# A graph network block on one core: the second attention layer's scores from weights times q and k, and an earlier fetch of swapped queries

## The reference, cut to what matters

```python
def _gate(h, q, Wg, bg, Wq, bq):
    ...
    attn = sigmoid(hg[:, :, None, :] + qg[:, None, :, :])      # hg: nodes, qg: queries
    qi = einsum('bnlf,blf->bnf', attn, q)
    alpha = sigmoid(h3 @ Wq[:, :F].T + qi @ Wq[:, F:].T + bq)
    return alpha * tanh(qi) + (1.0 - alpha) * h3

def rgat_conv(x, W, q, k, b, src, dst, etype, heads, out_ch, n_nodes):
    xr = einsum('nd,rdf->rnf', x, W)                           # three relations
    oi, oj = xr[etype, dst], xr[etype, src]
    alpha = leaky_relu(oi @ q + oj @ k, 0.2)
    a = softmax of alpha over the edges of each dst
    out = segment_sum(a * oj, dst)
    return out + b

h = elu(rgat_conv(x, W1, q1, k1, b1, ..., heads=4))
out = rgat_conv(h, W2, q2, k2, b2, ..., heads=1)
```

## Time and profile before

| | us |
|---|---|
| median of 3 runs | 279.88 (279.55 to 280.65) |
| the profiled execution's own time | 279.16 |
| its span in the trace | 277.4 |
| PE busy in the span | 255.4 (92%) |
| DVE busy | 146.9 (53%) |
| ACT busy | 91.6 (33%) |
| POOL busy | 85.5 (31%) |
| mean granted clock of TensorE | 0.994 of full speed |

### The profile page before, as it was taken

How to read it: one execution, slowest core, us unless ns; L and a number is a source line. 1 busy time by engine, 2 the same in 40 slices (tenths; PEclk the granted TensorE clock), 3 DMA queues, 4 the chain that set the end, 5 groups by cost and what they waited for, 6 DMA issues and landing times.

```text
span 277.4 us, 4929 instructions
## 1 busy us (share of the span) xinstructions
PE 255.4 (92%) x2073; PEld 132.2 (48%) x2073; DVE 146.9 (53%) x261; ACT 91.6 (33%) x155; POOL 85.5 (31%) x74
## 2 busy tenths in 40 slices
PE   8799999999899989899976998889999988998994
PEld 4566854455345532467752322225554443434572
DVE  1744640018999999730041999994632236114423
ACT  2312520034759986120001666771311022003000
POOL 7680000003999999100000668770000000000000
PEclk9999999999999999999997999999999999999999
DMA  7999996993007938004999600005999062000001
GB/s 238 374 402 402 402 390 195 409 401 121 1 0 263 402 95 270 0 2 144 408 296 392 239 4 2 0 2 169 377 405 398 18 233 110 0 2 0 2 0 28
DMA packets 21607, 52.67 MB, mean 190 GB/s; under 512 B 4169, under 2 KB 4937, under 8 KB 21586
## 3 DMA queue, kind: packets, MB, share of 16 engines
q1 hardware_dynamic: 20896, 52.04, 51.5%
q10 hardware_dynamic: 690, 0.34, 0.5%
HBM read 51.39 MB, written 0.20 MB: 186 GB/s over the span
## 4 chain that ended last, share of the span: by engine, by line
PE 54%; POOL 16%; DVE 10%; DMA 8%; issue 6%; ACT 4%; SPq 1%; DVEq 0%; POOLq 0%; ACTq 0%
POOL prod L591 12%; PE ps L1037 10%; PE ps L1069 9%; PE ps L1185 6%; PE ps L1457 6%; DMA W<-qg 4%; POOL W L591 4%; PE ps L1011 4%; PE ps L1084 4%; DMA W<-in_L_gnn_Wg 4%; PE ps L1154 2%; ACT pre L668 2%; DVE prod L877 2%; DVE pre L885 2%; PE ps L1275 2%
## 5 line engine op out<-in xcount | busy, mean ns | idle before, releaser
L591 POOL TENSOR_TENSOR prod<-pre,qn 128x768 f32<-128x768 f32 x28 | 56.0, 2021 | 17.0 <-ACT pre L668 16.9
L885 DVE TENSOR_TENSOR pre<-ps,qg 128x768 f32<-128x768 f32 x46 | 42.9, 949 | 7.4 <-PE ps L1261 6.3
L668 ACT ACTIVATE pre<-pre 128x768 f32<-128x768 f32 x46 | 38.7, 847 | 11.9 <-DVE pre L885 11.1
L1185 PE MATMUL ps<-W 128*128 128x384 f32 x96 | 34.4, 489 | 0.2 <-ACT W L443 0.2
L443 ACT COPY W<-ps 128x384 f32<-128x384 f32 x41 | 18.3, 482 | 38.9 <-PE ps L1011 38.7
L668 ACT ACTIVATE ps<-ps 128x768 f32<-128x768 f32 x18 | 14.3, 794 | 35.0 <-PE ps L1261 26.9
L1275 PE MATMUL ps<-prod,rsel 128*32 128x384 f32 x192 | 20.5, 496 | 3.4 <-POOL prod L591 2.5
L1185 PEld LDWEIGHTS ps<-W 128*128 128x128 f32 x96 | 17.4, 190 | 9.9 <-issue 0.9
L1069 PE MATMUL ps<-W,prod 128*64 128x256 f32 (+1 forms) x240 | 20.6, 328 | 0.0
L1011 PE MATMUL ps<-ident,W 128*128 128x128 f32 x144 | 19.3, 275 | 1.2 <-ACT W L443 0.7
L1011 PEld LDWEIGHTS ps<-ident,W 128*128 128x128 f32 x144 | 16.6, 141 | 4.7 <-issue 2.0
(11 more groups left out here) (203 smaller groups left out, 321.5 us busy)
## 6 DMA issues: line engine op xcount, KB each, us to landing
W<-in_L_gnn_W SPq DMA_DIRECT2D x9, 2304.0 KB, 11.8
W<-in_L_gnn_W_rel SPq DMA_DIRECT2D x6, 2304.0 KB, 15.3
W<-in_L_gnn_W_root SPq DMA_DIRECT2D x2, 2304.0 KB, 9.9
W<-in_L_gnn_Wq SPq DMA_DIRECT2D x4, 1152.0 KB, 7.9
W<-in_L_gnn_Wg SPq DMA_DIRECT2D x3, 1152.0 KB, 13.5
qn<-in_L_gnn_query_embs SPq DMA_DIRECT2D x4, 384.0 KB, 10.4
W<-in_L_gnn_Wg SPq DMA_DIRECT2D x3, 384.0 KB, 3.9
W<-qg SPq DMA_DIRECT2D x2, 384.0 KB, 10.9
```

The source lines that it names most:

```text
L591: nc.gpsimd.tensor_tensor(prod_of(T), pre_of(T), qn[:, pair_and_node(t)[0], :], ALU.mult).then_inc(prod_p, 1)
L668: nc.scalar.activation(tile, tile, ACT.Sigmoid).then_inc(sig_ready, 1)
L885: nc.vector.tensor_tensor(dst, ring(T), by_half(qg[:, pair_and_node(T % TILES)[0], :]), ALU.add).then_inc(pre_ready, 1)
L1185: ins = nc.tensor.matmul(ps[:, unit_bank(u), 0:HD], qT[:, k, p * P:(p + 1) * P], WgT_q[:, k, c * HD:(c + 1) * HD], start=(k == 0), stop=(k ...
```

## The change

Three things change.

- **Swapped queries.** SP fetches `qs` after the first relation of the second round (`rgcn_done` of 5), ahead of `L2_W1_0` and `L1_W`, where before it came behind both and waited for a value of 7. For this `L2_W1_1` (and so `qs`) moves to slot 3, and `L1_W` and `L3_W1` to slot 5.
- **Weights times q and k made ahead.** The scores of RGAT layer 2 need x W_r q and x W_r k. The kernel now makes V = (W_r q, W_r k), 36 columns of 128 numbers (three relations, six row blocks, q or k), while the work between the second gate and RGAT layer 2 runs. Once the second gate is reduced, SP spreads the rows q2 and k2 over 128 partitions (`qk_rows`, 384 KB each). 22 columns are made by POOL, which multiplies a weight block [128, 768] by the spread row (into one of four buffers `vprod`), and ACT, which sums it (`sum_products`, five stages of 6, 4, 5, 2 and 5). 14 are made by DVE in one instruction each (`v_units`, four stages of 4, 3, 5 and 2). The two small strided transfers of q2 and k2 go.
- **RGAT layer 2.** It is written out after a loop that now runs once. PE waits for V, multiplies it with `nodeT` and has q and k terms without `XT`; the scores and the softmax then run between the parts of the projection. The attention product is added in PSUM to bias and input (`RGAT2`), half by half, and the statistics are read from there.

```diff
-            ("L1_W", 3, 1), ("L2_W1_0", 2, 1), ("L2_W1_1", 5, 1), ("L2_W1_2", 6, 1),
-            ("L2_W2_0", 4, 1), ("L2_W2_1", 0, 1), ("L2_W2_2", 1, 1), ("L3_W1", 3, 1), ("L3_W2", 2, 1)]
+            ("L1_W", 5, 1), ("L2_W1_0", 2, 1), ("L2_W1_1", 3, 1), ("L2_W1_2", 6, 1),
+            ("L2_W2_0", 4, 1), ("L2_W2_1", 0, 1), ("L2_W2_2", 1, 1), ("L3_W1", 5, 1), ("L3_W2", 2, 1)]
...
+        V = prod[:, 3, 0:KC * R * GN].rearrange("p (k r c) -> p k r c", k=KC, r=R)
+        vprod = [pre[:, 2, :], pre[:, 3, :], prod[:, 0, :], prod[:, 1, :]]
 
         ps = ctx.enter_context(nc.psum_tensor("ps", [P, 8, 512], F32))
...
+        V_OF = {r: [(r, k, c) for k in range(KC) for c in range(2)] for r in range(R)}
+        ON_VECTOR = (4, 8, 2)
+        V_VECTOR = [V_OF[r][2 * KC - ON_VECTOR[r] + i] for r in range(R) for i in range(ON_VECTOR[r])]
+        V_POOL = [V_OF[r][i] for r in range(R) for i in range(2 * KC - ON_VECTOR[r])]
+        V_VECTOR_AT = (4, 3, 5, len(V_VECTOR) - 12)
+        V_SCALAR_AT = (6, 4, 5, 2, len(V_POOL) - 17)
+
+        def v_cell(unit):
+            r, k, c = unit
+            return V[:, k, r, c:c + 1]
+
+        def v_weights(unit):
+            r, k, c = unit
+            return W[SLOT[f"L2_W2_{r}"]][:, k, :]
...
-                sp.dma_start(qk[:, :, 1, q:q + 1], halves(a[f"L2_gnn_{name}2"]),
-                             allow_slow_non_contiguous=True).then_inc(qk_loaded, 16)
             done = R + 1
-            load("L1_W", a["L1_gnn_W"], rgcn_done, done + 1)
-            load("L2_W1_0", a["L2_gnn_W1"][0], rgcn_done, done + 2)
-            sp.wait_ge(rgcn_done, done + 3)
+            sp.wait_ge(rgcn_done, done + 1)
             for c in range(2):
                 sp.dma_start(qs[c * N:(c + 1) * N, :, :],
                              qg[(1 - c) * N:(2 - c) * N, :, c * HD:(c + 1) * HD]).then_inc(qs_loaded, 16)
+            load("L2_W1_0", a["L2_gnn_W1"][0], rgcn_done, done + 2)
+            load("L1_W", a["L1_gnn_W"], rgcn_done, done + 3)
             load("L2_W1_2", a["L2_gnn_W1"][2], rgcn_done, done + 4)
             load("L2_W2_0", a["L2_gnn_W2"][0], hg_done, 2)
-            load("L2_W1_1", a["L2_gnn_W1"][1], reduced, TILES)
+            sp.wait_ge(reduced, TILES)
+            for c, name in enumerate(("q", "k")):
+                sp.dma_start(qk_rows[c], a[f"L2_gnn_{name}2"].rearrange("f o -> o f").to_broadcast([P, D])).then_inc(qk_rows_loaded, 16)
+            load("L2_W1_1", a["L2_gnn_W1"][1])
...
+            pool.wait_ge(reduced, TILES)
+            nc.gpsimd.memset(prod[:, 3, 0:KC * R * GN], 0.0).then_inc(v_cleared, 1)
+            pool.wait_ge(qk_rows_loaded, 32)
+            for i, unit in enumerate(V_POOL):
+                wait_loaded(pool, f"L2_W2_{unit[0]}")
+                if i >= len(vprod):
+                    pool.wait_ge(v_sum_s, i - len(vprod) + 1)
+                nc.gpsimd.tensor_tensor(vprod[i % len(vprod)], v_weights(unit), qk_rows[unit[2]], ALU.mult).then_inc(v_product, 1)
...
+            def sum_products(stage):
+
+                for _ in range(V_SCALAR_AT[stage]):
+                    i = summed[0]
+                    act.wait_ge(v_cleared, 1)
+                    act.wait_ge(v_product, i + 1)
+                    nc.scalar.activation(vprod[i % len(vprod)], vprod[i % len(vprod)], ACT.Copy,
+                                         accum_out=v_cell(V_POOL[i])).then_inc(v_sum_s, 1)
+                    summed[0] = i + 1
+
...
+            sum_products(1)
...
+            sum_products(2)
...
+            sum_products(3)
...
+            sum_products(4)
...
+            def v_units(stage):
+
+                for _ in range(V_VECTOR_AT[stage]):
+                    unit = V_VECTOR[v_done[0]]
+                    dve.wait_ge(v_cleared, 1)
+                    dve.wait_ge(qk_rows_loaded, 32)
+                    wait_loaded(dve, f"L2_W2_{unit[0]}")
+                    if v_done[0]:
+                        dve.wait_ge(v_sum_v, v_done[0])
+                    nc.vector.tensor_tensor_reduce(vscratch[:, :], v_weights(unit), qk_rows[unit[2]], 1.0, 0.0,
+                                                   ALU.mult, ALU.add, v_cell(unit)).then_inc(v_sum_v, 1)
+                    v_done[0] += 1
+
             blocks_out(nodeT, node_turned, nodeT_ready, 3)
+            v_units(0)
             projection_norm(wide(GCN), xa[:, :], 2, 1)
...
+                v_units(1)
...
+                v_units(2)
...
+            blocks_out(nodeT, node_turned, nodeT_ready, 5)
+            v_units(3)
+            dve.wait_ge(rel_done, 4)
+            nc.vector.tensor_copy(X2[:, 0:HD], ps[0:N, 2, 0:HD]).then_inc(X_out_v, 1)
...
+            dve.wait_ge(rel_done, 7)
+            nc.vector.tensor_copy(X01[:, HD + CUT:D], wide(X1_WIDE)[:, CUT:HD]).then_inc(X_out_v, 1)
+            for part in range(2):
+                dve.wait_ge(att_part, part + 1)
+                stats(wide(RGAT2), part)
+            layer_norm(wide(RGAT2), xa[:, :], 3)
...
-                if layer == 1:
-                    ins = add_nodes(xa, ADDEND)
...
+            turn_nodes(hx, ident, node_turned, made=(x_ready, 4))
+            keep_warm(1, 4)
+            keys = [f"L2_W2_{r}" for r in range(R)]
+            project(nodeT, W[SLOT[keys[2]]], 2, waits=as_copied(nodeT_ready, 5)).then_inc(rel_done, 1)
...
+            def project_two(out_cols, bank, cols, blocks, last):
+
+                for k in blocks:
+                    h, j = k // JC, k % JC
+                    for r in range(2):
+                        ins = nc.tensor.matmul(bank[r * N:(r + 1) * N, out_cols], nodeT[:, j, h * N:(h + 1) * N],
+                                               W[SLOT[keys[r]]][:, k, cols], start=(k == BY_BLOCK[0]), stop=(k == BY_BLOCK[-1]),
...
+            first_half(BY_BLOCK[:2])
+            nc.tensor.matmul(ps[:, SCORE2, 0:n], ident[:, :], maskb[:, :], start=True, stop=False, skip_group_check=True)
+            pe.wait_ge(v_sum_s, len(V_POOL))
+            pe.wait_ge(v_sum_v, len(V_VECTOR))
+            for k in range(KC):
+                g, h, j = k % (P // GN), k // JC, k % JC
+                for r in range(R):
+                    ins = nc.tensor.matmul(ps[g * GN:(g + 1) * GN, QK2, r * N:(r + 1) * N], V[:, k, r, :],
+                                           nodeT[:, j, h * N:(h + 1) * N], start=(k == g and r == 0),
+                                           stop=(k + P // GN >= KC), skip_group_check=True)
+            ins.then_inc(qk_done, 1)
+            first_half(BY_BLOCK[2:4])
+            pe.wait_ge(qkT_ready, 2)
+            for half in range(2):
+                nc.tensor.matmul(ps[half * N:(half + 1) * N, SCORE2, 0:n], qsel[:, 1:2].to_broadcast([P, N]), QKT,
+                                 start=False, stop=False, skip_group_check=True)
+            for r in range(R):
+                for half in range(2):
+                    ins = nc.tensor.matmul(ps[half * N:(half + 1) * N, SCORE2, r * N:(r + 1) * N], QKT[:, r * N:(r + 1) * N],
+                                           qsel[:, 0:1].to_broadcast([P, N]), start=False, stop=True, skip_group_check=True)
+            ins.then_inc(score_done, 1)
+            first_half(BY_BLOCK[4:], True)
+            add_bias_wide("L2_gnn_b2", RGAT2)
+            add_nodes_wide(xa, RGAT2)
...
+            pe.wait_ge(wts_ready, 3)
+            nc.tensor.transpose(ps[:, WT1[0], 0:P], wts[:, 0:P], ident[:, :])
+            nc.tensor.transpose(ps[0:N, WT2[0], 0:P], wts[:, P:n], ident[:, :]).then_inc(wts_turned, 1)
+            second_half(0, BY_BLOCK[4:], True)
+            second_half(1, BY_BLOCK[:3])
+
+            def attend(half, part):
+
+                cols = PARTS_OF[part]
+                at = slice(half * HD + cols.start, half * HD + cols.stop)
+                for wT, X in ((wT1, X01), (wT2, X2)):
+                    ins = nc.tensor.matmul(wide(RGAT2)[half * N:(half + 1) * N, cols], wT[:, half * N:(half + 1) * N], X[:, at],
+                                           start=False, stop=(wT is wT2), skip_group_check=True)
+                return ins
+
+            pe.wait_ge(wT_out_s, 4)
+            pe.wait_ge(wT_out_v, 2)
+            pe.wait_ge(X_out_v, 3)
+            pe.wait_ge(X_out_s, 4)
+            for part in range(2):
+                attend(0, part)
+            second_half(1, BY_BLOCK[3:], True)
+            pe.wait_ge(X_out_s, 5)
+            attend(1, 0).then_inc(att_part, 1)
+            pe.wait_ge(X_out_v, 4)
+            attend(1, 1).then_inc(att_part, 1)
```

More of the change, by code:

```diff
@@ L141, in gnn_kernel @@
         RGCN2, HG1, GCN, LAST = 6, 4, 6, 4
+        X1_WIDE, RGAT2, QK2, SCORE2 = 6, 4, 5, 3
         SCORE = (0, 2)
@@ new lines, in _ @@
+            nc.scalar.copy(score[:, n:2 * n], ps[:, SCORE[1], 0:n]).then_inc(score_out, 1)
+            for h in range(2):
+                act.wait_ge(shifted, h + 1)
+                nc.scalar.activation(expd[:, h * n:(h + 1) * n], leaky[:, h * n:(h + 1) * n], ACT.Exp,
```

(19 more changed lines are left out.)

100 lines of the change are left out of this document (58 added, 42 removed).

## The result

The changed kernel takes 291.37 us (median of 4 executions, 290.97 to 291.57) against 280.26 for the kernel before beside it: a ratio of 1.0394, 95% interval 1.0361 to 1.0427. The forecast of 290.8 with its turns between POOL and DVE is what came. The profiled execution had 291.23 with a span of 289.4, which is 12.0 above the span before.

The account below looks back on a forecast made before the run. PE was taken to carry most of the chain, handing over in places, as in its 4.14 us wait for qs. 19.4 us lost less 8.5 gained is 10.9 slower than 279.16, plus 0.7 for the median: 290.8, range 278 to 298.

Parts of the forecast that it names:

- turns between POOL and DVE: Behind the second gate: whichever engine comes second waits for the other's whole instruction; 19.4 us lost, chance 0.70, range 285 to 297.
- Swapped queries: Before the second gate: PE's wait for qs (4.1 us) and its cold start go; 5.0 us gained, bounds 4.1 to 5.3.
- RGAT layer 2: Projection's start to last statistics: PE runs through, softmax hidden, 19.8 us where it was 23.3; 3.5 gained, bounds 2.5 to 4.5.
- step 5: Softmax of RGAT layer 1 and last stage: POOL's buffers are full, the last sums end before PE needs V; +0.
- Unhindered units: DVE's units without waiting for POOL: 0.7 us for the four units and 0.2 for the five.
- Step 1: First norm: L918 and L924, twice each, wait for POOL's first four products; 5.0 late or 0, taken as 3.5 us.
- Step 2: Four units behind the first norm's last copy, 2.55 us each between products after the first; +5.7 us, 0.7 without waiting.
- Step 3: Three units in the 3.82 us idle before the X2 copy: 2.4 too much, PE's other pairs hide part; +1.0 us.
- Step 4: Five units in the 5.03 us idle before RGAT layer 1's QKT copy take 12.7; +7.7 us, 0.2 without waiting.
- Step 6: PE idles over 5 us at the four and the five units, then runs some 3 us at half clock each; +1.5 us.
- No turns: Rival: units and short DVE instructions run at their own pace beside POOL; 272.3 us, chance 0.16; decided by units under 1.3.
- Mildly placed turns: Rival: rows land too late to hit the first norm and half the units meet no product; 279 to 283 us, chance 0.14.

Follow-up runs that it names:

- swap_only: The kernel before with only the early fetch of the swapped queries (new slots and SP's new order): 273.76 us, ratio 0.9754 to the kernel before.
- no_products: The changed kernel with each of POOL's 22 products replaced by a memset of one column, most of V wrong: 271.38 us, ratio 0.9668.
- no_units: The changed kernel without DVE's 14 units, 14 columns of V zero, POOL's products and ACT's sums kept: 281.02 us, ratio 1.0024.
- psum_row: The changed kernel with the second input of DVE's 14 units read from a PSUM bank, their columns of V wrong: 281.7 us, ratio 1.0041.
- half_units: The changed kernel with 7 of DVE's 14 units (2, 1, 3 and 1 per stage), 7 columns of V zero: 284.36 us, ratio 1.0166.
- softmax_pause: The changed kernel without DVE's units, and POOL waits before its 20th product until RGAT layer 1's softmax weights are ready: 279.67 us, ratio 1.0004.
- late_fills: The changed kernel with more filling matmuls on PE before the second norm's mean and RGAT layer 1's q and k terms: 289.92 us, ratio 1.0341.
- write_only: The changed kernel with each POOL product replaced by two memsets that write but read no SBUF, 22 columns of V zero: 271.62 us, ratio 0.9683.
- late_products: The changed kernel with POOL's products started only after the first norm has written both blocks, nothing left out: 288.91 us, ratio 1.0300.

## Why the prediction was right

Four kernels (before, swap_only, no_products and the changed one) can be set against each other on DVE's timeline. Each row counts from one milestone to the next, the first from the start of the span: the end of the first norm's aggregate (L861, L800 before), the end of `nodeT`'s last copy for L1 and for RGAT layer 1, the start of the `X2` copy, of the `QKT` copy and of `hx`, and the end of the span.

| us | before | swap_only | no_products | changed | turns |
|---|---|---|---|---|---|
| to the first aggregate | 197.50 | 192.03 | 192.30 | 194.70 | +2.4 |
| to `nodeT` for L1 | 3.41 | 3.40 | 3.40 | 6.49 | +3.1 |
| to `nodeT` for RGAT 1 | 8.44 | 8.43 | 8.77 | 14.70 | +5.9 |
| to `X2` | 3.82 | 3.83 | 3.83 | 5.88 | +2.1 |
| to `QKT` | 11.88 | 11.87 | 12.55 | 17.65 | +5.1 |
| to `hx` | 8.21 | 8.22 | 7.90 | 9.14 | +1.2 |
| to the end | 44.14 | 44.12 | 40.85 | 40.84 | 0.0 |
| span | 277.4 | 271.9 | 269.6 | 289.4 | +19.8 |

The last column is changed less no_products: what the turns cost, with what the clock makes of them. It was forecast at 18.5 (19.4 less the 0.9 of unhindered units).

- **Swapped queries**, forecast −5.0 with bounds of 4.1 and 5.3: −5.5 by the spans, just outside (and 6.6 by the medians, swap_only). PE asks for `qs` without a wait, and the node terms start at 145.71 where 145.8 was worked out.
- **RGAT layer 2**, forecast −3.5: −3.3 (44.14 to 40.84). The attention in two halves took 3.45 in the chain, forecast 3.7. From the projection's start to the third norm's statistics it is 19.6 us (249.90 to 269.54; 19.8 forecast); V was complete 2.5 us before PE asked for it (DVE's last unit ended at 253.2, V's product started at 255.7), so step 5's second half held.
- **Unhindered units**, forecast +0.9: +1.0. The span of no_products is 2.3 under that of swap_only, where layer 2 gives 3.3.
- **Step 1, the first norm**, forecast +3.5: +5.5, the largest loss beyond the forecast. The rows landed 5.6 us after their issue and not 3.9, so POOL's first product spared L979 and L985 the first time round, and the aggregate lost 2.4 only. But L871 behind it lost 2.6 (3.24 for two in place of 0.67). The step counted the instructions with two SBUF inputs and left out this one, which goes from SBUF to SBUF with one tensor input. That L871 was hit is chance of timing. In no_units, psum_row, half_units, softmax_pause and late_fills the rows landed earlier, three or four of the four were held up, and POOL had no free buffer when L871 came, so it took 0.67. The norm's last copy still came 4.5 us (softmax_pause) to 6.7 us (no_units) after that of no_products: the step's size holds on the whole, and which instructions pay for it changes with when the rows land.
- **Step 2, four units**, forecast 5.0 above unhindered ones: +5.9. Each took 2.29 to 2.60, and the four with their spaces 10.1 us; 9.4 was the sum, since it let the first one slip in after 1.6.
- **Step 3, three units**, forecast +1.0: +2.1. The copy of `X2` was expected 2.4 late, and came 2.1 late: the first unit took 0.95 and the two others 2.49 each with their spaces, against 1.05 and twice 2.55. The step then let PE, busy with other work, hide 1.4 of it. That happened in late_fills, where 1.2 are made good between `X2` and `XT`; in the changed kernel PE itself came out of its idle time at the lower clock, took 5.94 for the projection that takes 4.0, and hid nothing. ACT's copy of the same result, which has no unit before it, could not start before 221.77 either: the slow projection alone would have cost as much as the units did.
- **Step 4, five units**, forecast +7.5 above unhindered ones: +5.1. The five took 10.9 us in place of 12.7, since the first one came ahead of a product and took 1.03, and the third 1.95. Most of the rest is that unhindered they would have cost 0.7 (11.88 to 12.55 in the table) and not 0.2.
- **Step 5, the softmax**, forecast 0: +1.2. It met no product (L1041 took 0.36 twice), and what it lost is PE at its lower clock after 5.39 idle us.
- **Step 6, the clock**, forecast +1.5 (0 to 4) on its own, from over 5 us of idle PE in steps 2 and 4. In step 4 it was 5.39, in step 2 only 3.18, and the clock fell before either: PE idled for 2.13 us ahead of the first norm's mean, and the granted clock is 0.50 from 196 to 205 us, where no_products has 1.00. The L1 projection took 6.00 us there beside the four units, which hid it. The table has it inside steps 2 to 5, mostly in what step 3 didn't hide and in the softmax (1.2 each); late_fills puts the part behind the first norm at 1.4 by the medians and 2.5 in the profile.

The misses have both signs and cancel: +2.0, +0.9, +1.1, −2.4, +1.2 and −1.5 (step 6, which the other rows hold) make 1.3 of turns, and with −0.5 of the swap, +0.2 of layer 2 and 0.1 of units 1.1: 12.0 of span where 10.9 was forecast. The forecast of 290.8 is nearer still since the median stands 0.1 over the profiled execution here and not 0.7. So that it came within 0.6 us is luck in part; what the single steps bear out is the sum to a few us.

**Was it the mechanism?** Three independent removals say so: without POOL's reads (no_products, write_only) the units take 0.957 and 0.959 at the median, with one input moved to PSUM 0.954, and 2.294 with both. The Trainium skill states the rule in "SBUF — State Buffer", section Who interferes with whom: two SBUF inputs of VectorE contend with a GpSimd instruction that reads SBUF, not with one that only writes it. These runs agree, for the multiply-and-sum too. The same section says that `tensor_scalar` can enter modes of two ports, when its operands meet their conditions, and then contend with GpSimd. L871's 3.24 against 0.67 agrees, and so does its 1.17 beside memsets (write_only); in late_products the same operation from PSUM took 0.86 for two beside a busy POOL, as it does beside an idle one.

**The rivals.** "No turns" fails by 2.294 against the 1.3 us at which it would have decided, and its number, 272.3, is near that of no_products (271.38). "Mildly placed turns" (279 to 283) happens only with the units out or on PSUM (281.02 and 281.7).

## What to carry to other kernels

An engine with nothing to do is not a free one: before POOL gets SBUF-to-SBUF work, list each instruction of DVE on the chain beside it that has two SBUF inputs, or goes from SBUF to SBUF by `tensor_scalar`, and add up to a whole POOL instruction for each (the units here took 1.34 us longer at the median, beside products of 1.82). An operand in PSUM takes that price away; so does a POOL instruction that only writes, but not for the `tensor_scalar` from SBUF to SBUF (0.5 us for two in write_only). A wait of 2 us ahead of PE can cost 4 (4.3 in no_units), since PE comes out of it at half its clock. And measure the independent parts of a change alone: here one of them was worth 2.5% (273.76 us) and lay hidden under another that cost 6%.

## What was not expected of the hardware

- A `tensor_scalar` of two columns waited for POOL as the large ones do: 1.16 us for 0.16 (softmax_pause).
- A DVE instruction that came second did not always get the next turn: 2.40 us for 0.36 at 228.61 in no_units, the rest of one product and the whole of the next.
- ACT's sum of 768 columns is two instructions, 0.83 and a read of the accumulator of 0.19, 0.92 from start to end; four in a row started 0.83 apart (195.82 to 198.30), since the read overlaps the next.
- Spreading a row over 128 partitions (384 KB) took 3.6 and 5.6 us from issue to landing for two issued 0.4 apart, against 3.9 for a plain transfer of that size. A weight load of 2.3 MB was issued right behind them, so it isn't shown that the spreading is what takes longer.
- Kernels in which POOL reads all the time and DVE meets it only now and then (no_units, psum_row, softmax_pause) differ by 2.4 to 3.9 us over ten executions; those with few or no collisions (swap_only, no_products, write_only) by 0.2 to 0.4 over four. Collisions are not shown to be the cause: the kernel before, which has none behind its gates, differs by 2.6 to 3.3 over 13 executions, and late_products, which has many, by 0.2 over four.
